# Attention over edges: one source tile for each block of 128 edges, four sums handed over bank by bank, tile numbers read once for four groups

## What is computed

```python
h = node_feats @ W                      # 2500 x 128
s_l, s_r = h @ a_l, h @ a_r             # one score per node
logits = s_l[src] + s_r[dst]            # 40000 edges
e = exp(-leaky_relu(logits, 0.2))
row_sum = segment_sum(e, src, num_segments=N)
h_prime = segment_sum(e[:, None] * h[dst], src, num_segments=N)
return elu(h_prime / row_sum[:, None])
```

## Time and profile before

| | us |
|---|---|
| median of 3 runs | 2638.91 |
| lowest and highest run | 2629.41, 2640.44 |
| the profiled execution, its own time | 2631.99 |
| its span in the trace | 2630.2 |

### The profile page before, as it was taken

One profiled execution on the slowest core, in us unless ns is written; L12 is line 12 of the kernel. 1 busy time (PEld: TensorE's weight loads), 2 busy tenths in 40 slices (PEclk: granted clock), 3 DMA queues, 4 the chain that ended last, 5 costly groups with the idle time before them and its releaser, 6 DMA issues. The chain is left out here.

```text
span 2630.2 us, 47174 instructions
## 1 busy us (share of the span) xinstructions
PE 2039.4 (78%) x13095; PEld 1782.2 (68%) x13096; DVE 1533.2 (58%) x4828; ACT 1280.4 (49%) x2705; POOL 1322.9 (50%) x1131
## 2 busy tenths in 40 slices
PE   2499999999999999983647999995346666661978
PEld 2488888888888888873646888884334445441866
DVE  5377776776656556553554444444655555546873
ACT  1266665556655655651214565562146666651321
POOL 1288887788877777771001111113367777770000
PEclk9799999999999999996858999998678877875988
DMA  6566666666666666654106777774233333351001
GB/s 166 139 134 135 139 132 131 132 132 136 138 135 122 134 131 126 134 104 94 40 0 206 238 243 239 246 245 133 72 99 105 104 105 104 104 92 35 1 10 39
DMA packets 186005, 325.77 MB, mean 124 GB/s; under 512 B 27528, under 2 KB 109037, under 8 KB 185192
## 3 DMA queue, kind: packets, MB, share of 16 engines
q0 software_dynamic: 82080, 141.73, 26.8%
q1 hardware_dynamic: 102962, 181.83, 23.0%
q10 hardware_dynamic: 900, 1.50, 0.2%
HBM read 260.65 MB, written 64.30 MB: 124 GB/s over the span
## 5 line engine op out<-in xcount | busy, mean ns | idle before, releaser
L643 POOL DMA_INDIRECT edge_sums<-edge_agg,edge_slot x316 | 528.4, 1672 | 149.4 <-issue 82.8
L634 POOL DMA_INDIRECT edge_nf<-node_table,edge_node_idx x316 | 341.4, 1080 | 173.9 <-issue 84.4
L1764 POOL DMA_INDIRECT att_got<-head_table,att_idx x352 | 338.6, 962 | 125.1 <-issue 86.3
L474 PE MATMUL edge_e_ps<-edge_w_high,edge_hid_low 128*128 128x256 f32 x1264 | 369.7, 292 | 36.7 <-DVE edge_pre L839 22.2
L834 DVE TENSOR_TENSOR edge_hid_low<-edge_whole,edge_hid_high 128x512 fp32r<-128x512 f32 x316 | 216.3, 690 | 309.1 <-ACT edge_hid_high L776 308.8
L475 PE MATMUL edge_e_ps<-edge_w_low,edge_hid_high 128*128 128x256 f32 x1264 | 353.8, 280 | 0.0
L476 PE MATMUL edge_e_ps<-edge_w_high,edge_hid_high 128*128 128x256 f32 x1264 | 353.6, 280 | 0.0
L474 PEld LDWEIGHTS edge_e_ps<-edge_w_high,edge_hid_low 128*128 128x128 f32 x1264 | 241.4, 191 | 56.9 <-DVE edge_hid_low L834 28.8
L789 ACT ACTIVATE edge_agg<-edge_s_ps 128x1024 f32<-128x1024 f32 x79 | 81.1, 1026 | 391.6 <-PE edge_s_ps L716 353.6
L474 PE MATMUL edge_h_ps<-edge_eat_high,edge_w_low 128*128 128x512 f32 x632 | 252.3, 399 | 24.4 <-DVE edge_eat_low L830 23.6
L1798 PE MATMUL att_s_ps<-att_w,att_hot 128*125 128x258 f32 x704 | 246.1, 511 | 9.6 <-DVE att_hot L1876 9.6
(11 more groups left out here) (343 smaller groups left out, 4312.0 us busy)
## 6 DMA issues: line engine op xcount, KB each, us to landing
moe_w<-in_L_ffn_w_dram SPq DMA_DIRECT2D x162, 512.0 KB, 4.8
edge_ea<-in_edge_attr_dram SPq DMA_DIRECT2D x77, 448.0 KB
edge_dst_row<-dst_rows SPq DMA_DIRECT2D x79, 256.0 KB, 4.5
routed<-moe_out SPq DMA_DIRECT2D x54, 128.0 KB, 6.2
att_got<-head_table,att_idx POOLq DMA_INDIRECT x352
edge_nf<-node_table,edge_node_idx POOLq DMA_INDIRECT x316
edge_sums<-edge_agg,edge_slot POOLq DMA_INDIRECT x316
edge_ea<-in_edge_attr_dram SPq DMA_DIRECT2D x77, 64.0 KB
```

The lines of the kernel that those rows point to most:

```text
L474: pe.matmul(out, ll, rh, start=start, stop=False)
L634: pool.indirect_dma_start(nf[u][:, j, :], None, m.node_table[:, :], bass.IndirectOffsetOnAxis(ap=node_idx[u][:, j:j + 1], axis=0)).then_in ...
L643: pool.indirect_dma_start(m.sums[k][:, :], bass.IndirectOffsetOnAxis(ap=slot[u][:, j:j + 1], axis=0), agg[u][:, j, :], None, compute_op=AL ...
L1764: pool.indirect_dma_start(got[v][:, j, :], None, m.head_table[:, :], bass.IndirectOffsetOnAxis(ap=idx[v][:, j:j + 1], axis=0)).then_inc(la ...
```

## The change

A unit of the sort is now one block of 128 slots (`P`) in place of 256. So each block has its own tile, fewer slots stay empty, and there are `SRC_BLOCKS` = 336 blocks in place of 352: 84 groups, 21 turns. The tile row has 336 numbers in place of 176.

Two blocks can no longer share a sum. `scatter` writes each block's product into a bank of its own, and `accumulate` adds four banks for a group in place of two. PSUM has room for one set of four banks, `s_ps`, in place of two sets of two. It is handed over bank by bank: PE may write bank j of group g when DVE has added bank j of group g-1, and DVE may add bank j of group g as soon as PE has written it; `scattered` and `added` count single banks.

The tile numbers are read once for a turn, 16 in a row, at its beginning, in place of two for each group. This holds for PE and for DVE.

```diff
-PAIR = 2 * P
-PAIR_BLOCKS = -(-((N_EDGES + TILES * (PAIR - 1)) // PAIR * 2) // (2 * GROUP)) * 2 * GROUP
+SRC_BLOCKS = -(-((N_EDGES + TILES * (P - 1)) // P) // (4 * GROUP)) * 4 * GROUP
...
-    def tiles_of(eng, g):
-        return [eng.value_load(r.tile_row[0:1, bass.DynSlice(g * UN + n, 1)], min_val=0, max_val=TILES - 1) for n in range(UN)]
+    def tiles_of(eng, first, some):
+        return [eng.value_load(r.tile_row[0:1, bass.DynSlice(first * G + n, 1)], min_val=0, max_val=TILES - 1) for n in range(some * G)]
...
-        s_ps = [ps(f"s_ps{u}", [P, UN, 512]) for u in range(2)]
+        s_ps = ps("s_ps", [P, G, 512])
...
-                def scatter(g, u, wait_added=True):
+                def scatter(g, u):
                     pe.wait_ge(hot_ready, g + 1)
                     pe.wait_ge(scaled, g + 1)
-                    if wait_added:
-                        pe.wait_ge(added, (g - 1) * UN)
                     for j in range(G):
-                        last = nc.tensor.matmul(s_ps[u][0:LANES, j * UN // G, 0:ROW], hot[u][:, j, :], w[u][:, j, :],
-                                                start=j % (G // UN) == 0, stop=j % (G // UN) == G // UN - 1)
-                    last.then_inc(scattered, 1)
...
+                        if begun(g, 1):
+                            pe.wait_ge(added, g * G + (j - G + 1))
+                        nc.tensor.matmul(s_ps[0:LANES, j, 0:ROW], hot[u][:, j, :], w[u][:, j, :], start=True, stop=True).then_inc(scattered, 1)
+
+                def one_turn(g, ahead=RB):
+                    tiles = tiles_of(pe, g + 1, ahead)
+                    for v in range(RB):
+                        u = v % 2
+                        if left(g + v, 1, groups):
+                            source_scores(g + v + 1, 1 - u, tiles[v * G:(v + 1) * G])
+                        if left(g + v, 2, groups):
+                            turn_hots(g + v + 2, u)
+                        scatter(g + v, u)
...
-                def accumulate(g, u, first=False):
-                    tiles = tiles_of(dve, g)
-                    dve.wait_ge(scattered, g + 1)
+                def accumulate(g, tiles):
                     for n, tile in enumerate(tiles):
-                        if not first or n > 0:
-                            dve.wait_ge(added, g * UN + n)
-                        dve.tensor_tensor(acc[:, tile, :], s_ps[u][0:LANES, n, 0:ROW], acc[:, tile, :], ALU.add).then_inc(added, 1)
+                        dve.wait_ge(scattered, g * G + (n + 1))
+                        if begun(g, 1) or n > 0:
+                            dve.wait_ge(added, g * G + n)
+                        dve.tensor_tensor(acc[:, tile, :], s_ps[0:LANES, n, 0:ROW], acc[:, tile, :], ALU.add).then_inc(added, 1)
...
+                def one_turn(g, start=False):
+                    tiles = tiles_of(dve, 0, RB - 1) if start else tiles_of(dve, g - 1, RB)
```

More of the change, by code:

```diff
@@ L128, in __init__ @@
         self.ones = sb("ones", [P, P])
-        self.count_i = sb("count_i", [P, PAIR_BLOCKS], I32)
-        self.count = sb("count", [P, PAIR_BLOCKS])
-        self.count16 = sb("count16", [P, PAIR_BLOCKS], F16)
+        self.count_i = sb("count_i", [P, SRC_BLOCKS], I32)
+        self.count = sb("count", [P, SRC_BLOCKS])
+        self.count16 = sb("count16", [P, SRC_BLOCKS], F16)
         self.ident16 = sb("ident16", [P, P], BF16)
@@ L1725, in attend_edges @@
     G = GROUP
-    UN = G * P // PAIR
-    groups = PAIR_BLOCKS // G
+    groups = SRC_BLOCKS // G
     turns = groups // RB
     assert groups % RB == 0
-    def tiles_of(eng, g):
-        return [eng.value_load(r.tile_row[0:1, bass.DynSlice(g * UN + n, 1)], min_val=0, max_val=TILES - 1) for n in range(UN)]
+    def tiles_of(eng, first, some):
+        return [eng.value_load(r.tile_row[0:1, bass.DynSlice(first * G + n, 1)], min_val=0, max_val=TILES - 1) for n in range(some * G)]
     with ExitStack() as ctx:
@@ L1810, in _ @@
                 turn_hots(0, 0)
-                source_scores(0, 0)
+                source_scores(0, 0, tiles_of(pe, 0, 1))
                 turn_hots(1, 1)
-                for v in range(RB):
-                    one_group(v, v)
+                one_turn(0)
                 with pe.Fori(1, turns - 1) as i:
[L1816 to L1819, removed]
+                    one_turn(RB * i)
@@ L1821, in _ @@
+                one_turn(groups - RB, ahead=RB - 1)
             @block.scalar
@@ L1890, in logits @@
                     nc.vector.scalar_tensor_tensor(lrelu[u][:], z[u][:], NEG_SLOPE, z[u][:], ALU.mult, ALU.max).then_inc(lrelu_ready, 1)
-                def accumulate(g, u, first=False):
-                    tiles = tiles_of(dve, g)
-                    dve.wait_ge(scattered, g + 1)
+                def accumulate(g, tiles):
                     for n, tile in enumerate(tiles):
-                        if not first or n > 0:
-                            dve.wait_ge(added, g * UN + n)
-                        dve.tensor_tensor(acc[:, tile, :], s_ps[u][0:LANES, n, 0:ROW], acc[:, tile, :], ALU.add).then_inc(added, 1)
[L1900 to L1911, removed]
+                        dve.wait_ge(scattered, g * G + (n + 1))
[4 more added lines that the diff above has]
+                    tiles = tiles_of(dve, 0, RB - 1) if start else tiles_of(dve, g - 1, RB)
+                    for v in range(RB):
+                        u = v % 2
+                        if left(g + v, 2, groups):
+                            one_hots(g + v + 2, u)
+                        if left(g + v, RB, groups):
+                            stage_idx(g + v + RB, v)
+                        if left(g + v, 1, groups):
+                            logits(g + v + 1, 1 - u, (v + 1) % RB)
+                        if not (start and v == 0):
+                            k = v - start
+                            accumulate(g + v - 1, tiles[k * G:(k + 1) * G])
+                        if left(g + v, 1, groups):
+                            one_hots_whole(g + v + 1, 1 - u)
                 zeroed = sem("att_acc_zeroed")
@@ L1921, in _ @@
                 logits(0, 0, 0)
-                for v in range(RB):
-                    one_group(v, v, first=v == 1, start=v == 0)
+                one_turn(0, start=True)
                 with dve.Fori(1, turns - 1) as i:
[L1925 to L1929, removed]
+                    one_turn(RB * i)
+                one_turn(groups - RB)
+                accumulate(groups - 1, tiles_of(dve, groups - 1, 1))
 def attention_out(nc, sem, m, acc):
```

24 lines of the change are left out of this document (8 added, 16 removed).

## The result

The changed kernel takes 2805.78 us (median of 4 runs, 2803.17 to 2814.27) against 2639.68 us of the kernel before (4 runs). The ratio is 1.064, 95% interval 1.061 to 1.068. The prediction was 2790 us in a range of 2745 to 2850.

A forecast was written before the change was run, and what follows sets the result against it. The prediction took POOL's gathers to bound the attention over edges, with DVE the next bound and the new one after the change: 2632 + 115 + 91 - 61 - 8 + 25 - 4 = 2790 us, range 2745 to 2850.

The forecast's parts named there:

- What bounds it now: Attention over edges: POOL issues gathers without pause, 5.05 us a group; DVE is next with 4.45 us of work.
- Loads: DVE's tile-number reads: 160 more at 0.72 us each, one after the other, +115 us, bounds +91 and +118.
- the rival of the cheap batch: Tile-number loads in a row overlap, 3.6 us a turn, so about 2610 us and faster; chance 5%.
- PE's loads: PE's 16 tile-number reads a turn lie beside DVE's and count nothing; +10 us if cover failed by 0.5 us a turn.
- Additions: DVE's additions into the sums: 336 in place of 176, 160 more at 0.57 us each, +91 us.
- The wait for gathered rows: DVE's wait for POOL's gathers goes, as POOL is no longer the bound: -61 us, other end -43.
- The hand-over: PE-to-DVE bank exchange: DVE waits 1.0 us for scores in a group at half clock; +25 us, bounds 0 and +63.
- Four groups fewer: Denser packing saves DVE's other work in the attention stage, 4 x 1.98 us: -8 us.
- Elsewhere: Outside the attention stage: the placing's 640 matmuls lose 16 of 352 columns, -4 us; wider numbering operations taken as 0.
- The rival of the hand-over: With one bank set PE and DVE take turns, 1.0 us in every group outside a turn's beginning: 2838 us; chance 20%.

The follow-up runs named there:

- The kernel before with one load a turn: The kernel before, with the 8 tile numbers of a turn read by one unchecked load on PE and DVE: 2631.07 us, ratio 0.9985 to the kernel before.
- one wait for four: The changed kernel, but DVE waits once for a group's whole scatter before its four additions: 2807.21 us, 1.065 to the kernel before; run again, 2837.86 us.
- the kernel with one load: The changed kernel, with a turn's 16 tile numbers read by one load without range checks: 2604.53 us, ratio 0.988 to the kernel before.

## Why the prediction was right

*What bounds it now.* POOL's gathers did, with DVE next. The kernel before with one load a turn shows it: some 4 us of idle time a turn less on DVE for its loads (142.1 us ahead of the additions became 20.0 there and 32.3 at the turns' heads), and the same time.

*Loads.* The step was right, and so was the price of one load, 0.72 us from start to start. The term was a little too big, +115 predicted and +98 measured, mostly because `one_hots_whole` lies over the first load of a turn, about 0.5 us in each of 20 turns. That loads in a row do not overlap is shown by their starts and by the two kernels that drop the checks or the single loads; the rival of the cheap batch is out, since even without checks 16 loads take 6.4 us, and this rival needed 3.6. The floor of some 600 ns in the Trainium skill (DMA: Bandwidth & Descriptors, "Latency and other measured facts") was not seen: unchecked loads start 0.4 us apart. Unrolling does not spread their cost here; one load with 16 registers does.

*PE's loads.* That they lie beside DVE's is shown by both sides: without DVE's loads the wait for scores takes their place, and spread over the groups they no longer lie side by side and cost 185 us. But counting them at nothing was wrong. I had them start 0.9 us ahead of DVE's; they start 0.2 us behind, since DVE's sequencer loads while `one_hots_whole` still runs, and each takes 0.04 us longer. So they stick out by 0.71 to 0.83 us a turn, more than the 0.5 us that I kept as a bound: +14 us, predicted 0.

*Additions.* This term was mis-sized: +91 predicted, +117 measured. I took 0.57 us from a pair in the kernel before; in the change the wait for each bank (`scattered`) is a second wait ahead of each addition, and the pitch is 0.64. With one wait for four it is 0.57 again, though the time then goes into the wait for scores. That makes 18 of the 26 us. A gap of 0.08 us ahead of each group's first addition makes 7, and 2.3 are the last four loads, which stand there.

*The wait for gathered rows* went as predicted (the 61.2 us under the gathers are gone), and POOL waits for `idx` as foretold.

*The hand-over* was priced too high: +25 predicted, and the waits for scores outside the turns' heads are 3.7 us. I had DVE wait 1.0 us in a group at half clock. In the change such a group has 0.10 on average and at most 0.35; the one shown above has 0.21. With a pitch of 0.64 bank 0 is free 2.0 us before the end of the fourth addition and not 1.7, and the score matmuls start 0.2 us before the scatter's recorded end, where I had put them behind it. The slower additions thus hid the hand-over; with quicker ones it shows, as with one wait.

*Four groups fewer* was to save 8 us of DVE's other work. It did not show: DVE's busy time without the additions is 169.3 us before (1938.8 to 2387) and 171.7 after (1937.0 to 2562.5). *Elsewhere*, -4 was predicted and -4 measured, though 7.9 us of the first turn's loads are in that figure.

The direction and the main causes are thus shown, but the closeness of the sum, 16 us low, is partly luck: additions, PE's loads and the other work came out 26, 14 and 10 us above their terms and the gaps ahead of `att_z` 5, while loads and hand-over came out 17 and 21 below. The ends of the range were not the stacked bounds either; all low bounds together give 2741 us, all high ones 2849.

*The rival of the hand-over* did not come about, though its condition did in part: the granted clock of the stage fell from 0.78 to 0.73. But one wait for four additions brings it about in the groups with slow scatters, and handing the banks over as one set costs 138 us.

## What to carry to other kernels

Idle time under "issue" on an engine that reads numbers at run time is a cost like any other: look at the sequencer's rows, and count loads, checks and register operations at their full recorded time. Read several numbers with one load, clamp them where they are made rather than check them at each read, and if they must be single, put them where both engines stand still together. A packing that saves work on the bounding engine gains only as long as what it adds elsewhere stays under that engine's pace: 16 gathers fewer were worth 1.2% with cheap loads and cost 6.4% with dear ones.

## What was not expected of the hardware

How long one load of several numbers takes differs between two kernels by more than their count. 16 numbers are recorded with 1.10 us in the kernel with one load, yet 8 numbers in the kernel before with one load a turn with 1.85 us on DVE and 1.94 on PE; a single number takes 0.30.

```profile
L1732 PEldq TENSOR_LOAD <-slots_by_src_tile_row x23: 725/1935/1947, 1928.0 to 2357.8; - x23
L1732 DVEq TENSOR_LOAD <-slots_by_src_tile_row x23: 530/1847/1886, 1930.3 to 2383.1; - x23
```

The last loads, which stand outside the loop, have other counts. In the kernel with one load PE's last reads 12 numbers and DVE's last 4 (0.35 us, the lowest of the x22 above); in the other kernel PE's last reads 6 and DVE's last 2 (0.53 us, the lowest of the x23). PE's last load in each:

```profile
L1732 PEldq TENSOR_LOAD <-slots_by_src_tile_row x1: 855/855/855, 2336.5 to 2336.5; - x1
L1732 PEldq TENSOR_LOAD <-slots_by_src_tile_row x1: 1477/1477/1477, 2357.8 to 2357.8; - x1
```

So 4, 12 and 16 numbers take 0.35, 0.86 and 1.10 us in the one, 0.06 us for each further number, and 2, 6 and 8 take 0.53, 1.48 and 1.85 to 1.94 in the other, about 0.23 for each. Within a kernel the time follows the count; between them the price of a number is four times as high. The reads differ in their place in the tile row: they start at a multiple of 4 in the first kernel, and in the other at an even number that is not one. Whether that is the cause was not tried.
